# One step per FFN tile, a banded convolution on TensorE, and sampling on whole rows in a two-layer MetaFormer kernel

## The reference

```python
x = x + L0_conv(ln_c(x))              # deformable attention on depthwise convolutions
t = tokens(x);  t = t + moe_ffn(ln_t(t))
x = x + L1_conv(ln_c(x))              # sum of five depthwise convolutions
t = tokens(x);  t = t + moe_ffn(ln_t(t))

def L0_conv(x):
    value, query = dw3x3(x, w_v), dw3x3(x, w_q)
    key, off = dw3x3(x, w_k, stride=2), dw3x3(x, w_off1, stride=2)
    off = gelu(layernorm(off) * g + b)                 # over channels
    pos = tanh(off @ w_off2 + ref)                     # 28 x 28 sampling points
    v = grid_sample_bilinear(value, pos)
    attn = einsum('bcm,bcn->bmn', query, key) * 32**-0.5   # 12 groups of 32 (batch, channels)
    return w_out @ einsum('bmn,bcn->bcm', attn, v)
def L1_conv(x):                                        # depthwise, padded to the same size
    return dw7x7(x) + dw5x3(x) + dw3x5(x) + dw7x1(dw1x7(x)) + dw5x1(dw1x5(x)) + bias
def moe_ffn(x):                                        # 4 experts, the best 2 by softmax
    gates = top2_normalised(softmax(x @ gate_w + gate_b))
    return sum(gates[e] * (gelu(x @ w1[e] + b1[e], exact) @ w2[e] + b2[e]) for e in 4)
```

## Time and profile before

| | |
|---|---|
| median of three runs | 1856.06 us |
| the profiled execution | 1861.07 us |
| its span, first to last instruction | 1859.3 us |
| mean granted TensorE clock | 0.911 |
| busy: TensorE, VectorE, ScalarE, GpSimd | 75%, 72%, 39%, 16% |
| first GELU of FFN images 0, 1, 2, 3 | 383.5, 597.7, 813.4, 1015.1 us |
| first GELU of FFN images 4, 5, 6, 7 | 1209.5, 1404.5, 1586.7, 1727.9 us |
| bytes by DMA | 137.66 MB, 74 GB/s mean |

### The profile page before, as it was taken

One profiled execution on the slowest core, in us unless ns is written; L12 is line 12 of the kernel. 1 busy time (PEld: TensorE's weight loads), 2 busy tenths in 40 slices (PEclk: granted clock), 3 DMA queues, 4 the chain that ended last, 5 costly groups with the idle time before them and its releaser, 6 DMA issues.

```text
span 1859.3 us, 21000 instructions
## 1 busy us (share of the span) xinstructions
PE 1400.2 (75%) x5452; PEld 890.5 (48%) x5452; DVE 1346.9 (72%) x3073; ACT 724.0 (39%) x1436; POOL 303.3 (16%) x304
## 2 busy tenths in 40 slices
PE   2121623469879787787997899869987998899898
PEld 1010222335545454545554565546654665566565
DVE  1689398448874698547999799979998899443332
ACT  2130223225543354433444344434444344455443
POOL 1014013301150013201121112202121001000000
PEclk9999955589899899898998899989998999899999
DMA  2522213132421425123121421142213111221111
GB/s 66 130 53 59 74 45 90 37 109 68 118 75 30 139 67 145 56 83 93 58 62 42 149 68 56 45 146 61 66 49 113 45 52 42 79 70 60 53 59 48
DMA packets 105037, 137.66 MB, mean 74 GB/s; under 512 B 46070, under 2 KB 97144, under 8 KB 104184
## 3 DMA queue, kind: packets, MB, share of 16 engines
q1 hardware_dynamic: 98344, 131.20, 24.0%
q0 software_dynamic: 3072, 4.82, 1.1%
q10 hardware_dynamic: 3536, 0.63, 0.2%
HBM read 96.99 MB, written 39.62 MB: 73 GB/s over the span
## 4 chain that ended last, share of the span: by engine, by line
PE 32%; DVE 29%; issue 8%; POOL 6%; ACT 3%; DMA 1%; DVEq 1%; ACTq 0%; POOLq 0%
PE y_ps L815 15%; DVE acc L1106 9%; DVE part L1020 4%; PE h_ps L833 3%; PE h_ps L835 3%; PE h_ps L834 3%; POOL ln_rstd L730 3%; PE at_ps L920 3%; DVE ln_stats L994 3%; ACT ln_tok L598 2%; PE at_ps L851 2%; DVE pair L1026 2%; POOL ln_bias L733 2%; DVE ln_mv L1001 2%; PE lb_ps L794 1%
## 5 line engine op out<-in xcount | busy, mean ns | idle before, releaser
L629 ACT ACTIVATE hidden<-h_ps,b 128x448 f32<-128x448 f32 x672 | 421.5, 636 | 625.5 <-PE h_ps L835 619.5
L815 PE MATMUL y_ps<-hidden,w 128*96 128x448 f32 x1344 | 647.0, 567 | 19.1 <-ACT hidden L629 18.7
L1106 DVE SCALAR_TENSOR_TENSOR acc<-xq,all_w,acc 128x756 f32<-128x756 f32 (+2 forms) x504 | 475.9, 998 | 10.4 <-DMA xq<-norm_c 10.4
L833 PE MATMUL h_ps<-xh,w1h 96*128 96x448 f32 (+1 forms) x672 | 474.7, 706 | 0.0
L730 POOL TENSOR_TENSOR ln_rstd<-ln_ve,minus_half 112x4 f32<-112x4 f32 x112 | 154.7, 1382 | 1370.8 <-DVE ln_ve L1005 1362.7
L1020 DVE SCALAR_TENSOR_TENSOR part<-y_ps,b,gate_t 96x448 f32<-96x448 f32 x224 | 151.7, 677 | 298.9 <-PE y_ps L815 265.1
L794 PE MATMUL lb_ps<-ident,ln_tok 112*96 112x112 f32 x448 | 80.0, 312 | 332.5 <-ACT ln_tok L598 332.5
L598 ACT ACTIVATE ln_tok<-lt_ps,ln_bias,ln_rstd 112x96 f32<-112x96 f32 x448 | 156.3, 429 | 356.1 <-POOL ln_bias L733 332.1
L815 PEld LDWEIGHTS y_ps<-hidden,w 128*96 128x96 f32 x1344 | 211.2, 170 | 138.7 <-ACT hidden L629 52.7
L834 PE MATMUL h_ps<-xl,w1h 96*128 96x448 f32 (+1 forms) x672 | 251.0, 374 | 0.0
L835 PE MATMUL h_ps<-xh,w1l 96*128 96x448 f32 (+1 forms) x672 | 250.0, 372 | 0.0
(11 more groups left out here) (114 smaller groups left out, 1133.0 us busy)
## 6 DMA issues: line engine op xcount, KB each, us to landing
gate_t<-gates_dram SPq DMA_DIRECT2D x112, 336.0 KB, 3.3
xq<-norm_c SPq DMA_DIRECT2D x16, 420.0 KB, 4.9
xq<-norm_a SPq DMA_DIRECT2D x16, 336.0 KB, 4.1
ln_x_c<-in_x SPq DMA_DIRECT2D x28, 168.0 KB, 2.4
norm_a<-ln_cm_c SPq DMA_DIRECT2D x28, 168.0 KB, 2.0
x_res<-in_x SPq DMA_DIRECT2D x4, 1176.0 KB, 9.5
value_pairs<-pixels SPq DMA_DIRECT2D x4, 1176.0 KB
x_attn<-x_res SPq DMA_DIRECT2D x4, 1176.0 KB, 6.2
```

The lines of the kernel that those rows point to most:

```text
L629: act.activation(hidden[c % HID_RING][:, :], h_ps[c % H_BANKS][:, 0:TILE], ACT.Gelu, bias=b1[l][:, c:c + 1]).then_inc(gelu_done, 1)
L815: pe.matmul(y_ps[e % Y_BANKS][0:C, 0:TILE], w2[l][:, c, :], hidden[c % HID_RING][:, :], start=(j == 0), stop=(j == CPE - 1)).then_inc(hid_ ...
L833: pe.matmul(ps, hi, xh[:, cols], start=True, stop=False)
L1106: step(g, dve.scalar_tensor_tensor(dst, src, w, dst, ALU.mult, ALU.add))
```

## The change

- **Steps.** The program is a list of steps, one per FFN tile, all unrolled: one, then 14 ahead of the first FFN image, then 56. A step has two norm jobs (`place` 0 and 1): in tiles 0 to 2 of a period six of kind "c", in tiles 3 to 5 six of kind "f" for the next image, in tile 6 one of each. A job's input and result alternate between two buffers; the job of place 1 is turned back in the next step. `xh` and `xl` become a ring of eight tiles.
- **Attention** starts in tile 3 of a period, two periods ahead of its image's FFN, and ends in tile 2 of the next; all eight outputs are in stage 6, and each quarter is stored when it is ready. ScalarE issues its load, after GELU 4 of the step in which its taps begin.
- **The convolution** is made on TensorE alone. The channels are 16 groups of six (`xt`: partition = channel and row of a band of 20 rows; columns = 4 bands of 56 pixels). For each group and each of seven column offsets there is a 120 x 84 matrix with the taps of a column in bands (`toep`), made once in tile 3 of FFN image 2. An image takes eight fills of `at_ps` with 14 matmuls, three matmuls a chunk, from chunk 2 of tile 4 of one FFN image to chunk 7 of tile 1 of the next; VectorE adds each fill and the bias to the input (`add_fill`). The loads of `xt` are 24 DMAs on ScalarE's queue; input and result in this layout are 6 DMAs each on SP's.
- **Sampling** is done on whole rows: products and sums over 768 elements with the weight broadcast, seven instructions in place of 32 of 96 elements.
- **Gates**: the scores are read and the exponentials taken in the last tile of the image before; turning and storing them is still at the start of the image.

```diff
-    dict(ffn=0, lnf=1, lnc=("a", 3), attn=2),
+STEPS = [(-3, 6)] + [(period, p) for period in range(-2, 2 * NB) for p in range(TILES)]
+    if _p <= 2 and c_image(_period) is not None:
+        _todo = [("c", c_image(_period), 2 * _p + 1), ("c", c_image(_period), 2 * _p + 2)]
+    if 3 <= _p <= 5 and f_image(_period) is not None:
+        _todo = [("f", f_image(_period), 2 * _p - 6), ("f", f_image(_period), 2 * _p - 5)]
+    if _p == 6:
+        _todo = [("f", f_image(_period), 6), ("c", c_image(_period + 1), 0)]
+def attn_stage(period, p):
+    b = in_range(period + 2, NB) if p >= 3 else in_range(period + 1, NB)
+    return (b, p - 3 if p >= 3 else p + 4) if b is not None else (None, None)
+def conv_chunk(period, p, c):
+    at = p * CHUNKS + c - FILL_STEP * CHUNKS - FILL_CHUNK
+    for b, i in ((period - 2, at), (period - 3, at + TILES * CHUNKS)):
+        if in_range(b, NB) is not None and 0 <= i < FILLS * FILL_PITCH:
+            return b, i // FILL_PITCH, i % FILL_PITCH
```

On TensorE:

```diff
-                def middle_column(m, dy):
...
-                    ins = pe.matmul(at_ps[:, 0:YCOL], diag[:, g, dy, :], xq[:, g, at:at + YCOL],
-                                    start=(dy == 0), stop=(dy == 6))
+            def conv_fill(b, f, i):
+                if i == 0:
+                    pe.wait_ge(at_free, AT_CONV + FILLS * b + f)
+                    if f == 0:
+                        pe.wait_ge(xt_ld, 16 * CG * BANDS * (b + 1))
+                for n in range(FILL_MM * i, min(14, FILL_MM * (i + 1))):
+                    g, dx = 2 * f + n // 7, (3, 0, 1, 2, 4, 5, 6)[n % 7]
+                    x0, x1 = max(0, 3 - dx), SIDE - max(0, dx - 3)
+                    ps = at_ps[0:K_OUT, g % 2 * XCOLS:(g % 2 + 1) * XCOLS].rearrange("p (r x) -> p r x", x=SIDE)
+                    last = pe.matmul(ps[:, :, x0:x1], toep(g, dx), xt[:, g, :, x0 + dx - 3:x1 + dx - 3],
+                                     start=(n % 7 == 0), stop=(n % 7 == 6))
```

On VectorE, the convolution's result, the wait at the head of an attention step, and the sampling:

```diff
-            def conv_taps(slot, m):
...
-                            step(g, dve.scalar_tensor_tensor(dst, src, w, dst, ALU.mult, ALU.add))
+            def add_fill(b, f):
+                dve.wait_ge(at_full, AT_CONV + FILLS * b + f + 1)
+                if f == 0:
+                    dve.wait_ge(acc_ld[b], 16 * CG)
+                for g in (2 * f, 2 * f + 1):
+                    ins = dve.scalar_tensor_tensor(acc[b % 2][:, g, :], at_ps[0:K_OUT, g % 2 * XCOLS:(g % 2 + 1) * XCOLS],
+                                                   bias_c[:, g:g + 1], acc[b % 2][:, g, :], ALU.add, ALU.add)
+                ins.then_inc(at_free, 1)
+                if ops and stage == 0:
+                    dve.wait_ge(xq_ld, 16 * Q * (b + 1))
-                                ins = dve.scalar_tensor_tensor(vt[:, h, q, :], corner[:, i, :],
-                                                               o_cw[:, k, i:i + 1], vt[:, h, q, :],
-                                                               ALU.mult, ALU.add)
+                for k in range(2):
+                    to = total if 2 * r + k == 0 else o_n[:, :, :]
+                    link(dve.tensor_tensor(to, corner(k), weight(k), ALU.mult))
+                    if 2 * r + k == 3:
+                        dve.tensor_tensor(vt, total.rearrange("p (h q) c -> p h q c", h=2),
+                                          o_n[:, :, :].rearrange("p (h q) c -> p h q c", h=2), ALU.add)
+                    elif 2 * r + k > 0:
+                        link(dve.tensor_tensor(total, total, o_n[:, :, :], ALU.add))
```

On ScalarE, the loads (before on SP, at the start of a slot) and the exponentials:

```diff
+            def load_band(b, r):
+                for i in range(CG):
+                    src = norm["c"][b].rearrange("(c g) (y x) -> c y g x", c=CG, x=SIDE)[i, r * QROWS:r * QROWS + BAND]
+                    act.dma_start(xt[i * BAND:(i + 1) * BAND, :, r, :], src).then_inc(xt_ld, 16)
+                    if p == 3 and in_range(period - 2, NB) is not None and 5 <= c < 5 + BANDS:
+                        load_band(period - 2, c - 5)
+                    if p == 6 and c == 10 and f_image(period) is not None:
+                        exp_scores(f_image(period))
```

More of the change, by code:

```diff
@@ L1 @@
 import math
+from collections import namedtuple
 from contextlib import ExitStack
@@ L1349, in _ @@
                     dve.wait_ge(taps_set, 1)
+                if stage == 4 and b == 0:
+                    prepare_weights()
 def _constants():
```

1452 lines of the change are left out of this document (738 added, 714 removed).

## The result

The changed kernel takes 1881.6 us (1876.6 to 1881.9, four runs) against 1856.1 us for the kernel before beside it: the ratio is 1.0128, 95% interval [1.0107, 1.0148]. It is 1.3% slower. The forecast was 1804 us and faster, with a range of 1745 to 1862 us. Its profiled execution has a span of 1880.1 us.

A forecast was written before the change was run, and what follows sets the result against it. VectorE's taps were taken to bound convolution tiles, TensorE only 1 or 2 us under. FFN start 316.8 plus images of 212, 208, 213.3, 191.2 twice, 190.3, 153.3 and 131.4 gave 1807.5, less 3.2: 1804 us; range 1745 to 1862.

The forecast's parts named there:

- Loads moved to ScalarE's queue: Band loads between GELUs: 24 issues of 0.45 us, costing 6 us per image; attention's late load 10 us for images 1 to 3.
- the band loads choke ScalarE: Rival, convolution's input loads: at 1.1 us per issue 21.8 us lost per image, 1867 us in all; chance 0.14.
- the issues hide: Rival, band loads on ScalarE: its sequencer issues them beside GELUs, 24 us less, 1780 us; chance 0.14.
- The prologue: Before FFN 0: image 1's attention need not end first, so FFN 0 starts at 316.8 us instead of 383.5.
- The late quarter load: Attention's load, issued by ScalarE after GELU 4 of the tile where its taps start: 10 us, bounds 4 and 12.
- Attention in the FFN images: Attention stages spread over FFN tiles 0 to 6: tile times sum to 208 us per image, against 215 before.
- the convolution's price: Convolution on TensorE: 0.365 us per matmul, 112 matmuls, 41 us per image, 13 more than before.
- steady tiles bound by TensorE: Sign: a tile with convolution lasts near 28.7 us with TensorE full in it.
- images 5 and 6 slower than before: Sign: FFN images 5 and 6 take longer, 190.3 and 153.3 us against 182.2 and 141.2.
- sampling worth nothing: Whole-row sampling in attention saves about 5 us of VectorE per image, counted 0 because VectorE waits for gathers there.
- three signs by which the forecast wanted to be found wrong: Steady convolution tiles not bound by TensorE, FFN starting after 340 us, or the last two stages' images faster than before.
- The boundary between images: First tile of each FFN image, gates made between images: 7 us, bounds 3 and 9, against 8.9 before.

The follow-up runs named there:

- experiment 6: experiment 4 with the six accumulator loads of images 1 to 3 issued two by two in tiles 4 to 6 of the image before: 1808.2 us, ratio 0.9711.
- experiment 1: Changed kernel with each of the 24 band loads in 20 pieces of 3584 bytes instead of 320 of 224 (other values): 1842.9 us, ratio 0.9916.
- experiment 2: Changed kernel with the 24 band loads issued by SyncE, after its other loads of tile 3, instead of ScalarE: 1848.8 us, ratio 0.9945.
- experiment 3: Changed kernel with the six accumulator loads of images 1 to 3 issued in tile 0 instead of tile 3: 1874.4 us, ratio 1.0093.
- experiment 5: experiment 4 with the accumulator loads of images 1 to 3 moved from tile 0 to tile 1, ahead of the FFN store: 1873.1 us, ratio 1.0078.
- experiment 4: experiment 3 with one band load after each chunk of tiles 2 and 3, each waiting only for norm tiles it reads: 1847.8 us, ratio 0.9942.
- experiment 7: Changed kernel with VectorE waiting for GpSimd's two operations in image 0's f norm jobs: 1872.2 us, ratio 1.0088.
- experiment 9: experiment 6 with VectorE's wait of experiment 7 and the earlier positions, tanh and quarter loads of experiment 8: 1785.5 us, ratio 0.9587.
- experiment 8: experiment 5 with the edit of experiment 7 and attention's position job, tanh and quarter loads earlier: 1851.3 us, ratio 0.9966.
- experiment 11: Changed kernel with the old sampling, 32 operations of 96 columns per image instead of 7 of 768 elements: 1881.4 us, ratio 1.0120.
- experiment 10: Changed kernel with three of the convolution's seven column offsets left out (other values): 1818.4 us, ratio 0.9788.

## Why the prediction was wrong

By the profiled execution the sum was 72.6 us too low (1807.5 against 1880.1), step by step:

| step | forecast | measured | error |
|---|---|---|---|
| start of FFN 0 | 316.8 | 327.5 | +10.7 |
| image 0, image 1 | 212, 208 | 217.2, 219.2 | +5.2, +11.2 |
| image 2 | 213.3 | 234.5 | +21.2 |
| images 3, 4, 5 | 191.2, 191.2, 190.3 | 200.5, 201.4, 200.9 | +9.3, +10.2, +10.6 |
| images 6, 7 | 153.3, 131.4 | 151.0, 127.9 | -2.3, -3.5 |

**The step that failed is "Loads moved to ScalarE's queue", its 6 us per image.** It took 0.45 us per issue from a row of three issues with nothing queued ahead of them. The loads cost at least 18 us per image: pacing them gave back 73.4 us in four images (experiment 6 against the changed kernel), where 24 were counted, an error of 49. Three things were wrong in it. First, the price of an issue is no property of the DMA alone: its median here is 0.51, but in every image the fifth to the thirteenth of the 24 take 0.9 to 5.0 us. Second, TensorE was counted at full clock, and its clock falls while it waits: 6.2 of the 22.8 us in tile 3. Third, the sum left out SyncE's half. The same change of layout turns the accumulator's load and the convolution's store into six DMAs of 896 pieces of 224 bytes each. With the band loads these are 18432 small pieces per image, 73728 in all, which is nearly the 75863 by which packets under 512 bytes grew. The accumulator's block fell into the very tile of the band loads. Experiments 1 and 2 show ScalarE's part (39 and 33 us, with the rest coming back in tile 4), experiments 3 and 5 what their meeting costs, experiments 4 and 6 that SyncE's block of six costs 12 to 13 us an image by itself ahead of the FFN's loads, and next to nothing in pairs in tiles 4 to 6.

The rival "the band loads choke ScalarE" named the right place and very nearly the right loss: 21.8 us per image, 1867 us. Its 1.1 us per issue is near the mean of 1.04 in tile 3 of image 3, though single issues ran from 0.28 to 3.12. That the total came so near is partly luck: it knew nothing of SyncE's block, the clock or the attention tiles. Its reason against itself (that rows of 1.1 and more had come only with many small pieces queued) was the wrong way to read them, since this change queues many small pieces too. It had deserved more than 0.14, and the range, which ended at 1862, left out the rival's own 1867. The rival "the issues hide" is refuted: a GELU waited 10.97 us for five issues, and TensorE 7.6 for that GELU.

The Trainium skill (DMA: Bandwidth & Descriptors, "Issuing engines are not separate DMA queues") calls the time of issuing "usually small relative to the DMA itself"; the 10.61 us above do not agree. Its other sentence there, that DMAs from all engines run on the same 16 DMA engines and interleave, does agree with experiment 3. The Trainium skill (Perfetto Trace Analysis, "DMA Instruction — HWDGE (DVE, Sync)") says that the recorded time of an issue holds the wait for the descriptor generator and the making of all descriptors, and that more of them may be made than its buffer holds; which of the two waits fills an issue of 5 us here, no run shows.

**The prologue.** The forecast of 316.8 lacked one thing: unrolled, the norm jobs of image 0 meet an unbroken row of VectorE taps, and GpSimd's power does not get through. Experiment 7 takes that away and FFN 0 starts at 318.1. The late quarter load was priced at 10 us; earlier loads bring the start to 311.6 in experiment 9, 6.5 of these 10.

**Attention in the FFN images** was 11.2 us low in image 1: tile 2 +6.6 (44.5 against 37.9), tile 3 +7.0, tiles 4 and 5 +4.0 together, tile 1 +2.1, tile 0 -3.5, tile 6 -4.9. In tile 2 TensorE is busy for 40.2 us at a clock of 0.92 and idle for 4.3. 3.4 of these are the part of its 5.6 us wait for the sampled second row that falls into the tile, 0.9 two waits for `add_y`. The forecast had that row in the tile before and TensorE at full clock; behind the wait the clock is 0.69 (609.5 to 614 us), which is part of the 2.3 by which the busy time was priced low. Experiments 8 and 11 shorten that wait by 2.4 us at most, so no run shows what the tile would be without it. In tile 3 earlier quarter loads gave 3.9 and 1.5 us (38.9 and 36.6 in experiment 5, 35.0 and 35.1 in experiment 8).

**Right were** the convolution's price (0.365 forecast, 0.37 in the timeline, 0.33 by experiment 10), steady tiles bound by TensorE (28.7 forecast, 28.1 and 27.4 measured), VectorE near 50%, images 5 and 6 slower than before, and sampling worth nothing, though for another reason than the one given (experiment 11). TensorE's share did not come to over 80% but to 77%. None of the three signs by which the forecast wanted to be found wrong came up: steady tiles are bound by TensorE, FFN starts before 340 us, and images 5 and 6 are slower. They did not look at the tile with the loads. The boundary between images was dear at 7 us: tile 0 of image 7 is 4.2 longer than tile 1, within the bounds of 3 and 9. Without the block loads an image beside the convolution is 181 to 182 us long, where 178.2 + 7 = 185.2 had been counted; experiment 6, with 1808 us, is close to the 1804 of the forecast partly by luck: against the sum, FFN 0 starts 12 us late and images 0 to 2 are 22 us longer, while images 3 to 5 lack the 18 us of loads that were counted and are 10 us shorter besides.

## What to carry to other kernels

When a change re-tiles an operand, count the pieces of every DMA that touches the new layout, stores and accumulators too, on all queues, and lay them on one time axis; the engine that issues them pays from a few issues on (here from the fifth of 320 pieces or the third of 896). Price an issue by rows with many pieces queued as well as by lone ones, and give the first as much chance as the block is long. Ask what the wait does to TensorE's clock. Spread such DMAs one or two at a time through the work of the issuing engine, each waiting only for the rows that it reads, and don't put them in a block ahead of loads with a date, that is, for which another engine will soon stand waiting.
